# Both halves of a unit's product with V issued after all four of its score matmuls, in two attentions of a transformer kernel

## What is computed

```python
x = x + attn_a(layernorm(x))      # 32 heads of 8, 1024 keys, biases
x = x + ffn(layernorm(x))
x = x + attn_b(layernorm(x))      # 32 query heads, 8 key/value heads, a band of 128 keys before the query masked
x = x + ffn(layernorm(x))
...
scores = einsum('bhqd,bhkd->bhqk', q, k) * scale
probs = softmax(scores, axis=-1)
ctx = einsum('bhqk,bhkd->bhqd', probs, v)
```

## Time and profile before

| | |
|---|---|
| median of 3 runs | 1661.97 us (1661.29 to 1664.39) |
| profiled execution, its own time | 1661.77 us |
| its span, first to last instruction | 1659.8 us |
| PE busy | 1609.1 us (97%), 14128 matmul records |
| DVE busy | 1491.0 us (90%) |
| ACT busy | 1281.8 us (77%) |
| granted TensorE clock, mean | 0.991 of full speed |

### The profile page before, as it was taken

The page is one execution under the profiler, slowest core; times in us unless marked ns, Lnnn a source line. Parts: engine busy times, 40 slices in busy tenths (PEclk is TensorE's granted clock), DMA queues, the critical chain, the costliest instruction groups (busy, mean ns, idle before and its releaser), DMA issues.

```text
span 1659.8 us, 39596 instructions
## 1 busy us (share of the span) xinstructions
PE 1609.1 (97%) x14128; PEld 636.9 (38%) x14128; DVE 1491.0 (90%) x2168; ACT 1281.8 (77%) x2424; POOL 266.8 (16%) x623
## 2 busy tenths in 40 slices
PE   6899999999999999999988999999999999999999
PEld 3322222222222223787653222222222222237877
DVE  6999999999999997787678999999999999937765
ACT  3399999999999998433224999999999999983321
POOL 1410000000000000000012222333332233320000
PEclk9989999999999999999998999999999999999999
DMA  6943344334354321200404232222222322112000
GB/s 160 296 98 70 63 76 84 63 64 84 69 139 87 73 60 44 64 1 0 117 15 132 59 66 57 51 51 65 57 55 62 62 57 51 55 49 58 14 13 26
DMA packets 72126, 114.70 MB, mean 69 GB/s; under 512 B 12464, under 2 KB 27824, under 8 KB 71984
## 3 DMA queue, kind: packets, MB, share of 16 engines
q1 hardware_dynamic: 71984, 112.63, 29.2%
HBM read 71.96 MB, written 40.63 MB: 68 GB/s over the span
## 4 chain that ended last, share of the span: by engine, by line
PE 54%; DVE 35%; issue 7%; ACT 1%; DMA 1%; SPq 0%; DVEq 0%; POOLq 0%; ACTq 0%
DVE mneg L1306 28%; PE psum L785 18%; PE psum L767 11%; PE psum L737 7%; PE psum L887 5%; PE psum L843 5%; PE psum L848 2%; PE psum L700 2%; PE psum L823 2%; PE psum L720 1%; PE psum L682 1%; DVE area L1356 1%; DVE area L1390 1%; DVE stats L1199 1%; DVE area L1340 1%
## 5 line engine op out<-in xcount | busy, mean ns | idle before, releaser
L1055 ACT ACTIVATE area<-psum 128x512 f32<-128x512 f32 x2048 | 1097.2, 600 | 42.1 <-PE psum L767 13.7
L785 PE MATMUL psum<-area 128*32 128x256 f32 x8192 | 655.2, 392 | 0.4 <-POOL area L1568 0.4
L767 PE MATMUL psum<-area 51*128 51x512 bf16 x2048 | 639.2, 385 | 2.5 <-DVE vsb_b L1256 1.4
L1312 DVE CUSTOM_DVE_ANT_0 xn<-psum,band 128x1024 f32<-128x1024 f32 x512 | 588.4, 1220 | 10.3 <-PE psum L737 9.3
L1306 DVE TENSOR_REDUCE mneg<-psum 128x1 f32<-128x1024 f32 x512 | 581.0, 1211 | 7.0 <-PE psum L737 6.9
L785 PEld LDWEIGHTS psum<-area 128*32 128x32 f32 x8192 | 162.1, 108 | 400.7 <-issue 259.1
L737 PE MATMUL psum<-area 48*128 48x512 bf16 x1024 | 301.6, 385 | 8.2 <-DVE mneg L1306 5.1
L767 PEld LDWEIGHTS psum<-area 51*128 51x128 bf16 x2048 | 141.0, 94 | 427.0 <-ACT area L1055 353.3
L737 PE MATMUL psum<-k_max_b,area 48*128 48x512 bf16 x1024 | 292.8, 385 | 5.4 <-DVE mneg L1312 4.7
L1549 POOL TENSOR_TENSOR mparts<-mneg,nought 128x16 bf16<-128x16 f32 x64 | 14.1, 221 | 742.3 <-DVE mneg L1306 501.1
L1100 ACT ACTIVATE area<-psum 128x512 f32<-128x512 f32 x64 | 38.2, 599 | 115.9 <-PE psum L848 115.8
(11 more groups left out here) (89 smaller groups left out, 1092.1 us busy)
## 6 DMA issues: line engine op xcount, KB each, us to landing
ctx_rows<-area SPq DMA_DIRECT2D x64, 256.0 KB, 2.1
area<-q_stacks SPq DMA_DIRECT2D x32, 384.0 KB, 6.8
area<-k_stacks SPq DMA_DIRECT2D x64, 192.0 KB, 5.6
area<-q_stacks_b SPq DMA_DIRECT2D x32, 384.0 KB, 5.3
area<-q_stacks SPq DMA_DIRECT2D x32, 192.0 KB, 4.6
area<-q_stacks_b SPq DMA_DIRECT2D x32, 192.0 KB, 3.4
area<-ctx_rows SPq DMA_DIRECT2D x16, 256.0 KB, 4.1
area<-inv_rows SPq DMA_DIRECT2D x16, 256.0 KB, 4.5
```

The lines of the kernel that those rows point to most:

```text
L767: pe.matmul(psum[:, BANK_OF["exp", g, u, head], :], k_st[lo:lo + ROWS + PARTS, buf, 0 if a else head // 2, kt * P:(kt + 1) * P], q_st[lo:l ...
L785: mm = pe.matmul(psum[head * VW:(head + 1) * VW, BANK_OF["ctx", g, qh], cols], vaug[:, buf, kt, head, :], probs[:, u % PRING, head, cols], ...
L1055: act.activation(probs[:, u % PRING, head, :], psum[:, BANK_OF["exp", like, u, head], :], ACT.Exp, scale=SCALE).then_inc(bank_freed, 1)
L1312: dve.tensor_tensor_reduce(band_out[:, c % 2, :], slot, band[:, at:at + SEQ], 1.0, -3.0e38, ALU.add, ALU.max, mneg[:, qh, col:col + 1]).th ...
```

## The change

In `group` on TensorE, S1 and S3 are issued as before, but V0 and V1 both go behind S3. The order of a unit is now S0, M, S1, S2, M, S3, V0, V1. It holds in both attentions and in all groups, also in the last one and its units without maxima. Since V0, which first needs a new ctx bank in units 2 and 10, now comes behind S3, `share_banks` takes that bank after head 3 instead of after head 1. No instruction is added or removed.

```diff
@@ share_banks
-                if head == 1 and u % BT == LAG and (g or u >= BT):
+                if head == GH - 1 and u % BT == LAG and (g or u >= BT):
                     taken.append(("ctx", g, u // BT))
@@ group (TensorE)
                         elif ahead:
                             max_scores(a, g + 1, 1 - buf, c - CHUNKS)
-                        if u < LAG and first:
-                            scores(a, g, buf, u, 2 * step + 1, ahead)
-                        else:
-                            scores(a, g, buf, u, 2 * step + 1, ahead)
-                            times_v(*of, step, ahead or u < LAG)
+                        scores(a, g, buf, u, 2 * step + 1, ahead)
+                    if u >= LAG or not first:
+                        for part in range(2):
+                            times_v(*of, part, ahead or u < LAG)
```

## The result

The changed kernel takes 1740.91 us (median of 4 runs, 1740.22 to 1744.23) against 1661.63 us (4 runs of the kernel before beside it): a ratio of 1.048, 95% interval 1.0459 to 1.050, so 4.8% slower. The forecast was 1737 us. The profiled execution's span is 1738.3 us, 78.5 us more than before.

The account below looks back on a forecast made before the run. VectorE's reductions were taken to bound the kernel, with TensorE close beside. 1661.8 + 36.6 + 30.0 (long stretches) + 4.0 + 4.3 (last groups) = 1736.7, so 1737 us, 4.5% slower; range 1710 to 1766 us.

Parts of the forecast that it names:

- VectorE's pace: Attentions before the change: reductions back to back, 1.131 and 1.145 us apart, set units of 2.262 and 2.290 us.
- TensorE runs close beside it: Attentions before the change: half a unit takes TensorE 1.12 us against VectorE's 1.131.
- The wait of S3: S3 needs the bank E0 frees, 1.09 us after S0; it would be there after 0.72, so waits 0.37 us.
- The unit: Middle groups after the change: 1.09 + 0.31 + 0.43 + 0.57 = 2.40 us from S0 to S0.
- Both stretches of 239 units: Long windows from group 0 to 15: 577.2 us each, +36.6 in the first attention and +30.0 in the second.
- The turn: Two in each group put 0.17 us ahead of S0, no longer hidden: +5.1 us over thirty.
- The last groups: From unit 3 of group 15 to the output projection: +4.0 us in the first attention, +4.3 in the second.
- The exchange of the ctx bank: In thirty units V0 waits for E0 behind the ctx copy: 1.33 us instead of 1.40, -0.08 each, -2.4 us.
- E0: ScalarE's exponential of S0's scores; at an exchange, forecast to start 0.47 us behind the ctx copy, last 0.63, release after 0.06.
- Its cycle isn't the bound: VectorE's reductions and M hold S3 till about 0.8 us after S0, less than 1.09, so add nothing.
- VectorE keeps the pace: Rival, 8%: S3 waits less, the unit falls to 2.26 us, time stays at 1662, plus 3 at most.
- The gain of the saved changes between scores and V: Rival, 3%: TensorE is the bound, two changes fewer save 0.2 us a unit, 48 us, giving 1614.

Follow-up runs that it names:

- half_max_before: The kernel before the change with half of the maxima left out (512 keys of each chunk): 1677.7 us, ratio 1.005.
- exp256_half_max: The changed kernel with each exponential over 256 of 512 columns and the maxima over half of the keys: 1632.2 us, ratio 0.983.
- half_max_after: The changed kernel with half of the maxima left out (512 keys of each chunk): 1740.2 us, ratio 1.048.
- exp256_after: The changed kernel with each exponential over 256 of its 512 columns, all maxima kept: 1710.8 us, ratio 1.030.
- exp384_after: The changed kernel with each exponential over 384 of its 512 columns, all maxima kept: 1717.5 us, ratio 1.034.
- five_banks_split: The changed kernel with half of the maxima left out, the freed bank given to the pool, and the old order in 14 of 16 units: 1642.8 us, ratio 0.988.

## Why the prediction was right

**The bound before.** VectorE's pace, 1.131 and 1.145 us a reduction, was read rightly: every one of them in groups 1 to 14 of the first attention is 1.13 us behind the last, and in the changed kernel they move to 1.209 us apart with the unit. That TensorE alone stands in the second attention's chain meant nothing. But "TensorE runs close beside it" was truer than I knew. I compared half a plain unit, 1.12 us, with 1.131; with exchanges and turns the old order needs 2.260 us a unit (`half_max_before`), 0.002 and 0.03 below VectorE's pace. A faster VectorE alone would have brought next to nothing in the first attention.

**The wait of S3.** Forecast 1.09 us from S0 to S3, measured 1.07 to 1.08. It falls to 0.86 with an exponential over half of the columns (`exp256_half_max`) and to 0.67 with a fifth bank. I took its pieces from rows that I had misnamed: the turn at 402.05 stands ahead of S0 of unit 13, so the matmuls at 400.93 and 401.17 are S2 and S3 of unit 12 and those at 402.22 and 402.50 are S0 and S1. The two halves of a unit are built alike, score, M, score, V, so the sum came out. The unit: forecast 2.40, measured 2.395. V0 to the next S0 took 1.00, as summed from 0.43 and 0.57. Both stretches of 239 units: forecast 577.2 us each, measured 578.4 and 581.0.

**Smaller terms.** The turn (+0.17) was right: 2.561 less 2.395. The last groups: forecast +4.0 and +4.3, measured +3.8 and +4.0. The exchange of the ctx bank was mis-sized. I took 0.08 us off each; in groups 1 to 14 it takes 2.408 us, 0.01 more than a plain unit. One of them, ScalarE and then TensorE, to be read beside the earlier trace rows:

```profile
397.91 0.58 ACT L1071 COPY area<-psum 128x512 f32<-128x512 f32 x1
398.40 0.60 ACT L1054 ACTIVATE area<-psum 128x512 f32<-128x512 f32 x1
```

```profile
397.78 0.39 PE L767 MATMUL psum<-area 51*128 51x512 bf16 x1
...
399.14 1.07 PE L785 MATMUL psum<-area 128*32 128x256 f32 x16
```

The copy starts 0.13 us behind S0 (taken: 0.17) and E0 0.49 behind the copy (0.47), but V0 comes 0.14 us behind E0's end (399.00) and not 0.06. In groups 0 and 15, where ScalarE's code is written out, the exchange unit is 2.37 against 2.46 us and the 0.08 holds. What lengthens the release inside the loops stays open. The exchanges are some 2.6 us more than forecast in each attention and the plain units, 0.005 us shorter than 2.40, some 1.1 us less: the 1.2 us by which the first stretch exceeds the forecast is what two errors of opposite sign leave.

**"Its cycle isn't the bound."** This step was right for the changed kernel as it is, and in the second attention barely so. The round of the maxima is a second limit, 579 us there against 581.0 measured, and 554 against 578.4 in the first: in the second attention the changed kernel's units show it (2.43 us for unit 11, 2.63 with the turn after unit 4, against 2.40 and 2.56 in `half_max_after`), about 0.15 us a group and 2 us in all, part of the 3.8 us by which that stretch exceeds the forecast. Shorten the exponential and it takes over (`exp256_after`, `exp384_after`). My rival "VectorE keeps the pace" said that a wait of S3 shorter by 0.14 us would cost nothing. That is wrong. With an exponential 0.21 us shorter 43 us of the loss remain.

**The rivals.** None held. The gain of the saved changes between scores and V exists, 0.24 us in a plain unit, and showed with four banks left for scores; with three the wait takes it back.

## What to carry to other kernels

When work on an in-order engine is moved to leave its fellows adjacent, count the buffers: with n banks in turn, n + 1 of the now adjacent instructions cannot be closer, first to last, than one whole round of writing, reading and releasing a bank. The moved work used to fill this round for nothing. Here one bank more turned 4.8% slower into 6.6% faster, in a kernel that leaves out half of the maxima to have it. Check the second-longest round too: in the second attention it stood 2 us below the first in 581, and so decided what a shorter exponential could bring; a total that agrees says nothing of it. And compare paces over a whole period, not over its plainest unit: the exchange and the turn used up the 0.04 us by which the plain unit was ahead in the first attention.

## What the runs showed of the hardware

The granted clock did not come back soon though TensorE had no idle time. In `half_max_before` PE is busy 10.00 of 10.00 us between 930 and 940 us at a clock of 0.50 (1.2 GHz), and the clock stays there for 64.9 us. In the kernel before the same place was over after 10.2 us. Leaving out half of the maxima is not enough to explain it: `half_max_after` leaves out the same half and has 10.2 and 23.9 us. The cause stays open. The Trainium skill, TensorE: Matmul & The Clock Gate, Part 1, has sustained matmul activity release the throttle. These rows agree that the clock comes back; a timeline without a gap did not bring it back within those 10 us.

The repeated runs of `half_max_before` spread over 54 us and those of `five_banks_split` over 45, where the changed kernel's spread over 4. The spread goes with the clock: the fastest run of `half_max_before` (1660.5 us) has a mean granted clock of 0.980, the slowest (1714.7) 0.945. So a time that rests on such a stretch is worth little without its clock rows.
